# Issuing the feed-forward weight loads from GpSimd's queue in place of SyncE's

## What is computed

```python
xn = layernorm(x)                                   # per row of 1024
q, k, v = split(xn @ w_qkv.T, 3)                    # 512 each
s = softmax(causal(q @ k.T * 512**-0.5)) @ v @ w_out.T + b_out
gate = xn @ (w_gate/127).T                          # w_gate, w_up: 3072 x 1024 int32
up   = xn @ (w_up/127).T
y    = (silu(gate) * up) @ (w_down/127).T           # w_down: 1024 x 3072 int32
out  = x + s * silu(y)
```

## Time and profile before

| what | us |
|---|---|
| median of the timed runs | 1818.64 |
| the profiled execution | 1826.93 |
| its slowest core, first to last instruction | 1825.4 |
| spans of its 8 cores | 1804.3 to 1825.4 |
| TensorE busy, of the span | 1629.5 (89%) |
| VectorE busy | 429.6 (24%) |
| ScalarE busy | 258.0 (14%) |
| GpSimd busy | 6.6 |
| first gate matmul of the feed-forward phase, from the span's start | 746.4 |

### The profile page before, as it was taken

One profiled execution on the slowest core, in us unless ns is written; L12 is line 12 of the kernel. 1 busy time (PEld: TensorE's weight loads), 2 busy tenths in 40 slices (PEclk: granted clock), 3 DMA queues, 4 the chain that ended last, 5 costly groups with the idle time before them and its releaser, 6 DMA issues.

```text
span 1825.4 us, 20552 instructions; the slowest of 8 cores (1804.3 to 1825.4 us)
## 1 busy us (share of the span) xinstructions
PE 1629.5 (89%) x7748; PEld 780.6 (43%) x7748; DVE 429.6 (24%) x740; ACT 258.0 (14%) x415; POOL 6.6 (0%) x16
## 2 busy tenths in 40 slices
PE   4788799968888888899999899999899998999995
PEld 3555544434444443344444344444344443444442
DVE  5333222132222222122200322201322102222102
ACT  2323211132222222101100110001011001010001
POOL 0000000000000000000000000000000000000000
PEclk9888899979999999899999999999899999999987
DMA  4112010014444430333422533423433424333323
GB/s 141 36 35 70 1 35 12 1 58 95 102 93 99 90 78 24 69 79 72 129 80 70 143 76 81 127 76 117 97 70 81 128 77 135 77 81 70 110 64 127
DMA packets 236113, 146.17 MB, mean 80 GB/s; under 512 B 202929, under 2 KB 211377, under 8 KB 235442
## 3 DMA queue, kind: packets, MB, share of 16 engines
q1 hardware_dynamic: 234674, 123.89, 25.6%
q0 software_dynamic: 768, 18.88, 5.8%
q10 hardware_dynamic: 576, 2.10, 0.4%
HBM read 146.94 MB, written 35.65 MB: 100 GB/s over the span
## 4 chain that ended last, share of the span: by engine, by line
PE 82%; DVE 6%; DMA 4%; ACT 4%; issue 2%; DVEq 1%; ACTq 0%; SPq 0%
PE psA L247 54%; PE psA L941 9%; PE psB L676 5%; PE psB L941 5%; PE psC L941 5%; PE psB L742 4%; DMA xin<-x 2%; DMA wub<-wub_scr 1%; DVE xnT_lo L448 1%; DVE otl L974 1%; DVE otl L971 1%; DMA wof_st<-woutT 1%; ACT oaT_hi L700 1%; ACT oaf L682 1%; ACT xnT_hi L441 1%
## 5 line engine op out<-in xcount | busy, mean ns | idle before, releaser
L247 PE MATMUL psA<-xnT_hi,wgb 128*128 128x512 f16 x768 | 296.4, 386 | 32.8 <-DMA wub<-wub_scr 30.8
L247 PE MATMUL psA<-xnT_lo,wgb 128*128 128x512 f16 x768 | 296.1, 386 | 0.0
L247 PE MATMUL psA<-xnT_hi,wub 128*128 128x512 f16 x768 | 291.1, 379 | 0.0
L247 PE MATMUL psA<-xnT_lo,wub 128*128 128x512 f16 x768 | 291.1, 379 | 0.0
L857 DVE SCALAR_TENSOR_TENSOR hfs<-psA,hsc 128x512 f32<-128x512 f32 x96 | 66.4, 692 | 476.7 <-PE psA L247 473.0
L849 ACT ACTIVATE hsc<-psA,zeroc 128x512 f32<-128x512 f32 x96 | 66.0, 688 | 596.4 <-PE psA L247 561.4
L247 PEld LDWEIGHTS psA<-xnT_hi,wgb 128*128 128x128 f16 x768 | 76.2, 99 | 129.8 <-issue 42.6
L941 PE MATMUL psA<-wdb,hT_hi 128*128 128x512 f16 x384 | 118.5, 391 | 11.7 <-DVEq L1007 10.9
L941 PE MATMUL psA<-wdb,hT_lo 128*128 128x512 f16 x384 | 119.8, 395 | 0.0
L247 PEld LDWEIGHTS psA<-xnT_lo,wgb 128*128 128x128 f16 x768 | 76.1, 99 | 92.8 <-issue 5.5
L247 PE MATMUL psA<-xnT_hi,wqh 128*128 128x512 f16 x256 | 101.1, 395 | 15.4 <-DVEq L1007 15.4
(11 more groups left out here) (109 smaller groups left out, 1655.8 us busy)
## 6 DMA issues: line engine op xcount, KB each, us to landing
wgb<-wgb_scr SPq DMA_DIRECT2D x96, 256.0 KB, 3.5
wub<-wub_scr SPq DMA_DIRECT2D x96, 256.0 KB, 4.0
wdb<-wdb_scr SPq DMA_DIRECT2D x96, 256.0 KB, 2.6
xt<-x SPq DMA_DIRECT2D x16, 512.0 KB, 3.9
sscr<-stl SPq DMA_DIRECT2D x16, 512.0 KB, 3.9
sin<-sscr SPq DMA_DIRECT2D x16, 512.0 KB, 5.6
xin<-x SPq DMA_DIRECT2D x16, 512.0 KB, 6.9
out<-otl SPq DMA_DIRECT2D x16, 512.0 KB, 3.4
```

The lines of the kernel that those rows point to most:

```text
L247: k.op("te", lambda e, lf=lf, rf=rf, j=j, n=n, pf=psum_ap_fn: e.matmul(pf(), lf(), rf(), start=(j == 0), stop=(j == n - 1)), inc=(inc if j ...
```

## The change

All loads of `wgb`, `wub` and `wdb`, and the waits ahead of them, move from SyncE's list to GpSimd's. GpSimd gets the two waits that start the feed-forward phase as well; SyncE keeps its own copies. Which buffer, which semaphore and which step is waited for stays the same. SyncE keeps the loads of sin and xin and the stores of out.

```diff
     k.wait("sy", "ve", ve_p2_done)
     k.wait("sy", "dG", 16 * 12)
+    k.wait("gp", "ve", ve_p2_done)
+    k.wait("gp", "dG", 16 * 12)
...
     def emit_gu_load(h):
         if pe_gu_use.get(h % 2) is not None:
-            k.wait("sy", "pe", pe_gu_use[h % 2])
-        k.dma("sy", lambda h=h: wgb.ap()[:, h % 2],
+            k.wait("gp", "pe", pe_gu_use[h % 2])
+        k.dma("gp", lambda h=h: wgb.ap()[:, h % 2],
               lambda h=h: wg_r[:, :, h * 128:(h + 1) * 128], f"dF{h % 2}")
-        k.dma("sy", lambda h=h: wub.ap()[:, h % 2],
+        k.dma("gp", lambda h=h: wub.ap()[:, h % 2],
               lambda h=h: wu_r[:, :, h * 128:(h + 1) * 128], f"dF{h % 2}")
...
                     if pe_wd_use.get(hh0) is not None:
-                        k.wait("sy", "pe", pe_wd_use[hh0])
-                    k.dma("sy", lambda hh0=hh0: wdb.ap()[:, hh0],
+                        k.wait("gp", "pe", pe_wd_use[hh0])
+                    k.dma("gp", lambda hh0=hh0: wdb.ap()[:, hh0],
                           lambda hh0=hh0: wd_r[:, hh0, :], f"dD{hh0}")
...
                 if pe_wd_use.get(h % 2) is not None:
-                    k.wait("sy", "pe", pe_wd_use[h % 2])
-                k.dma("sy", lambda h=h: wdb.ap()[:, h % 2],
+                    k.wait("gp", "pe", pe_wd_use[h % 2])
+                k.dma("gp", lambda h=h: wdb.ap()[:, h % 2],
                       lambda h=h: wd_r[:, h, :], f"dD{h % 2}")
```

## The result

The changed kernel takes 1832.2 us (median of 11 runs) where the kernel before takes 1818.6 in the same series; the ratio is 1.0082, 95% interval 1.0071 to 1.0093. It is slower by 0.8%, where the forecast was a gain, 1810: the stated range of 1797 to 2000 holds the time, but the sign is wrong.

What follows compares the result with a forecast made beforehand. TensorE was taken as the bound, so a load matters only if late. Slab starts 8.1, clock 2 and other waits 0.6 gained, phase start 2 and first pair 0.3 lost: 8.4 us off 1818.6, 1810; range 1797 to 2000.

Steps and rivals of the forecast that it cites:

- Part 1, slab starts: Starts of slabs 1 to 3: stalls shrink to 3.4 to 5.8 us, 8.1 us gained, plus 2 from less half-rate clock.
- Part 2, the start: Phase start, slab 0: sin and xin, 2 MB, issued at once beside the first weights; 2 us lost (0.5 to 3).
- Part 3, down: Down steps: wdb loads issued from GpSimd use 2.9 of a 3.24 us budget, so stay hidden; cost zero.
- Part 3, gate and up: Gate and up steps: the pair uses 5.6 of 6.3 us, hidden; only the first pair loses 0.3 us.
- G: GpSimd's generation time for one gate or up load: taken as about 1.2 us, pair fits below 1.55.
- The threshold in ns per packet: Gate and up: the pair fits if a packet beyond 64 costs GpSimd at most 1.1 ns, with 1042 packets a load.
- My guess that most of the 522 ns is start-up: GpSimd's issue: its existing small transfers hold it 522 ns each, judged mostly start-up; called the forecast's weak point.
- Rival 2: Every gate and up step: GpSimd's descriptor generation becomes the bound, slower from G = 1.55 us, 1890 at 2.0; chance 0.38.
- Rival 3: Down: loads late by 0.1 to 0.7 us in 88 steps, 9 to 60 us, 1811 to 1872; chance 0.06.
- Rival 1: Slab starts: the wait moves in full as VectorE's chain is pushed back, nothing gained, 1816 to 1821; chance 0.13.
- rival 4: Gate and up: VectorE's cast holds up GpSimd's generation, pairs 0.43 us later, at most 38 us, 1810 to 1848; chance 0.04.
- The sum: Whole kernel: 8.1 + 2 + 0.6 - 2 - 0.3 = 8.4 us off the median 1818.6, giving 1810.

Runs made afterwards that it cites:

- The gate: Changed kernel, but in slab 0 SyncE issues sin and xin only after the weight pairs of steps 0 and 1 have landed: ratio 1.0147, median span 1817.1 us.
- the common list: All weight loads, sin and xin in GpSimd's list, four wdb buffers, output tiles 2 and 3 finished in the next slab: ratio 0.9892 to before, span 1791.3 us.
- the alternating loads: Kernel before with odd wdb loads on GpSimd and even ones on SyncE; run once, for its profile: 1853.6 us.

## Why the prediction was wrong, step by step

- **Part 1, slab starts: right, but for the clock.** VectorE's chain takes over the wait, as forecast. Stalls of 4.47, 5.41 and 4.16 us on core 2, forecast 3.4 to 5.8; over all cores they are 3.2 to 7.3, median 4.2, where before had 6.7 to 9.7, median 7.9. The three gate and up parts are 8.1 shorter (8.8 by the medians), forecast 10.1 with the clock (8.1 + 2). The 2 us of clock did not come: the half-rate stretches after the stalls lasted 5.1, 5.0 and 2.9 us on core 2, where they had lasted 4.0, 5.3 and 3.3. The later xin was forecast too: 8.75 us on core 2 against 7.67.
- **Part 2, the start: right mechanism, mis-sized.** 2 us (0.5 to 3) was the term for 2 MB beside the first pair, 5.0 is the measured loss. I shared the rate of another stretch in equal parts. The rate was near (242 GB/s from 741.5 to 752.6 on core 0, for 262); the shares failed: some 2.7 of the 3.1 MB of sin, xin and both pairs had moved when the first pair had landed, where my sum has 1.0, and its landing is 10.06, not 4.9 + 2. The gate and the common list each bring it back to 4.4 to 5.3.
- **Part 3, down: the step that failed, and that turned the sign.** I wrote "budget 3.24, used 2.7", added 0.2 for the longer issue, got 2.9, and the landing did come out as 2.9. But a landing counts from the start of the issue. The budget has to begin at TensorE's signal, and from there to the issue GpSimd takes 0.50 us where SyncE takes 0.06: I had left SyncE's 0.07 in the sum for GpSimd. A load issued after step h is wanted by step h + 2, so the time of two steps must hold one step's matmuls to their end, 3.61 us (1.89 + 0.86 + 0.86), and the load's whole way. On the chain of core 2: 3.61 + 0.54 (925.84 to 926.38) + 2.93 + 0.14 = 7.22 us, where two steps take 6.90: 0.3 late in two steps, 0.16 in each. On SyncE it is 3.61 + 0.06 + 2.7 + 0.14 = 6.5, 0.4 to spare. My spare of 0.5 was read from 943.79 in the earlier trace rows, where a piece of the chain begins; the matmul that wants the load starts at 943.63 in TensorE's timeline. I had named this the thinnest cover in the kernel, and given its rival 0.06.
- **Part 3, gate and up: right.** G is 0.88 to 0.89 us, below my 1.2 and far below 1.55; the pair is hidden. The 24 steps of slab 0 take 171.3 us against 171.4. The threshold in ns per packet was badly posed: issued from GpSimd a gate or up load is not 1042 packets. It is (23808 - 768) / 288 = 80, and a wdb load is 80 too (with wdb alone on GpSimd its queue has 8448 packets, (8448 - 768) / 96). My guess that most of the 522 ns is start-up was right: 1024 pieces take only 366 ns more.
- **Rival 2** (0.38) did not happen. **Rival 3** (0.06) did, at its lower end: 0.14 to 0.16 us in 88 steps is 12 to 14 us, 15 by the medians over the cores, 1811 to 1872 forecast, 1832 measured. **Rival 1** and **4** did not, but see the cast.
- **The sum** by the measured terms on core 2: slab starts -8, start +5, down +13.5, 10.5 in all; by the medians over the cores -8.8, +5.0, +15.0, 11 in all. Forecast: -10.7, +2.3, 0.

The estimate from the Trainium skill, page DMA: Bandwidth & Descriptors (Latency and other measured facts), of 0.4 us more to the first byte from GpSimd is close to the 0.45 by which the runs show the issue delayed. I set it against the landing, which has 0.2 to 0.3 more of its own; the two together, some 0.7, are over the 0.4 us that was spare, by the 0.3 that the alternating loads show. The rule of the same page of the Trainium skill on issuing engines (Issuing engines are not separate DMA queues: their transfers share the same engines and interleave) holds here, and the runs add the order: a pair issued beside or behind the 2 MB of sin and xin lands late from the other queue (10.4 us) and from the same one (7.6 on SyncE, 10.5 on GpSimd), and what it costs hangs on how soon the pair is wanted.

## What to carry to other kernels

A budget for a load begins at the signal that frees its buffer, not at the issue; before a load moves to another engine's queue, price signal to issue on that engine, and give it more buffers where the cover is under a microsecond (four did it here; three were not tried). A list of transfers is an order of issue: splitting it frees what was blocked, and also everything that was rightly kept behind. And where two lists hold a wait in series, moving one gives only the difference to the other: here the emission order of two output tiles was worth 23 us, more than any choice of queue.

## What the runs showed of the hardware that I had not expected

- From a semaphore to the start of a DMA issue: 0.48 to 0.54 us on GpSimd, 0.05 to 0.06 on SyncE; 0.48 and 0.05 in the same execution, where the queues alternate.
- GpSimd's issue of 128 partitions by 8 pieces of 256 bytes takes 884 ns and of 128 by 2 KB 540; SyncE's 360 and 320.
- The same gate or up load is about 1042 packets from SyncE and 80 from GpSimd; a wdb load 144 and 80.
- VectorE's cast of 128x512 beside GpSimd's descriptor generation takes longer, while GpSimd's issue does not (882 to 953 ns in all 96 of wgb). VectorE's timeline of the changed kernel's core 0, with GpSimd busy and idle:

```profile
852.03 0.80 DVE L863 CAST hT_hi<-hfs 128x512 f16<-128x512 f32 x1
...
1032.40 0.43 DVE L863 CAST hT_hi<-hfs 128x512 f16<-128x512 f32 x1
```

  So rival 4's contest exists, with the loser exchanged: the cast went from 427 to 730 ns in the mean, which TensorE sees at the end of gate and up of slabs 0 to 2 (3.12, 3.01 and 3.01 us of wait for VectorE on core 2, before 2.77, 2.66 and 2.76), and not in the last slab (2.67 against 2.69), where GpSimd has no pair to issue for a next one. The Trainium skill, page SBUF — State Buffer (Who interferes with whom), states that whoever issues first has the shared port and the other blocks. The trace agrees on the direction: GpSimd issues first, from 851.71, and the cast at 852.03 is the one that takes longer. But it lasts only 0.37 longer though GpSimd generates for 1.76 us on end, so it was not held until the end.
